# V projected for two units at a time, in high and low parts, in the decoder's local-attention stack

## The chip, the cores and the metric

One core of a Trainium2 chip runs the whole program. The metric is the device time of one execution in microseconds (us), lower is better; the time before is the median of three runs.

## The reference

The program is one decoder step: a state-space and expert block, a cross attention, and then a stack of six layers. All of the change is in the stack. Cut to what matters, a layer of the stack is:

```python
def attn_layer(x, Wqkv, qs, ksc, Wo):            # x: (2, 512, 128), 16 heads of 64
    q, k, v = jnp.split(x @ Wqkv, 3, -1)         # each split in 16 heads
    q = l2norm(q) * qs; k = l2norm(k) * ksc
    q = q * cos * scale + rotate_half(q) * sin * scale
    k = k * cos * inv + rotate_half(k) * sin * inv
    out = local_attention(q, k, v)               # windows of 32, each looks at itself and the one before
    return out @ Wo

for i in range(6):
    x = attn_layer(shift_tokens(x), ...) + x
    x = ffn_layer(shift_tokens(x), ...) + x      # layer norm, a * gelu(gate), W2
```

`v = x @ Wv` is 512x128 by 128x1024 for each of the two sequences, in every layer. This product is what is computed in another way.

## The kernel before

Activations lie transposed, channels on the 128 partitions and the 512 positions of a sequence along the free dimension (`Y`, called `stream` in the trace). The work of a layer is cut in 16 units: unit n is sequence n // 8 and head pair n % 8. All engines run the same software pipeline, `body(s)`, one step t at a time (t = 0 to 15 in a layer; -4 to -1 fill it at the start). Each engine works through its own list in program order and waits on semaphores (`Flow`; `at(turn, n)` is the n-th event of a turn, which is a layer). In step t the engines do, among other things:

- TensorE (L1376): the scores of unit t+1 (L1299, L1305), the projection of Q and K for unit t+4 (`project`, L1254), the transposes of the probabilities of unit t (L1317), the output projection of unit t-1 (L1339), the V projection of unit t+1 (`project_v`, L1280), the sum of squares of the heads of t+4 (`head_norm`, L1273, into `NORM_BANK`), and probabilities times V of unit t (`values`, L1320).
- ScalarE (L1468): the squares of unit t+4 (L1420), the exponential, two copies of probabilities (L1451), the copy of V to SBUF (`copy_v`, L1453), logarithm and root of the norm, the copy of the output.
- VectorE (L1594): row maximum and subtraction (L1604, L1610), the multiplication with the norm (`normalise_heads`, L1550, output `st_turned`), in some steps the rounding of a weight (`high_weights`, L1527), in some steps parts of the feed-forward block, then the two rotary products (`rotate`, L1539, L1540), the row sum and the reciprocal (L1632, L1636).
- GpSimd, called POOL (L1658): the sum of two squares (L1667, output `st_sq_sum`, which `head_norm` waits for), the two rotary sums (L1671, L1672), the normalised probabilities (L1679, `pn`, shown as `mo_w<-st_prob,st_ri`, which the transposes of the next step wait for), and in some steps the low part of a weight (`low_weights`, L1654).
- SyncE (SP, L1215): the DMAs. `place_heads` puts Q (4 DMAs) or K (8 DMAs, `st_k_blocks`) of unit t+3 in place, `shift_values` makes a copy of V shifted by 32 positions, `st_vs`, with 2 DMAs for each unit; weights of the next layer are loaded in chosen steps.

Names in the trace are those of the buffers: `st_sq_sum`, `st_turned`, `st_w_high` and so on; `h` is `sq`, `x` with 128x1024 is `sin_part`, `mo_w` stands for `cos_part` and `pn`, which lie in a buffer of an earlier part, and `banks` is PSUM.

Q and K are projected in three passes of a faster one-pass format (`F32R`, fp32r in the trace): the weight and `Y` are each split in a rounded high part and the remainder, and high times high, low times high and high times low are added in PSUM (L1266 to L1270). The splitting of `w_raw` is done ahead, one eighth i in step t = i + 7 of the layer before (for the first layer in the steps -4 to 2): VectorE rounds (L1530), POOL subtracts (L1656). V is projected in plain fp32 from `Y` and `wv`, a unit at a time: four matmuls, each with 128 positions as output rows and 128 columns (L1290); the hardware runs each as two passes, so the trace shows eight.

The feed-forward block of one sequence lies in the steps 0 to 3 (for sequence 1 of the layer before) and 8 to 11 (for sequence 0): stage 0 adds the attention output (`residual1`, L1558) and takes the mean (L1343) and variance (L1347), stage 1 the first gate products, stage 2 the two value products L1369 ahead of the transposes, stage 3 the last products and `down` (L1374). It borrows `V_BANK` for some products, so `project_v` waits for `act_done` in the stages 2 and 3.

## Time and profile before

| what | value |
|---|---|
| median of 3 runs | 1370.93 us |
| lowest and highest of them | 1365.84 and 1378.49 us |
| the profiled execution's own time | 1366.57 us |
| its span, first to last instruction | 1363.8 us |
| the stack, first projection to the end of its pipeline | 395.2 to about 1320 us |
| TensorE busy | 1174.1 us (86%) |
| VectorE, ScalarE, POOL busy | 942.8, 838.3, 658.7 us |
| mean granted TensorE clock | 0.948 |

The time outside the span is 2.8 us in the profiled execution. The busy time of an engine is a sum over the whole program; whether an engine is the bound is read from what its neighbours wait for. A row of the timeline gives the start, the duration, the engine, the line, output <- input, and in brackets the idle time in front of it and what ended that.

### The profile page before, as it was taken

Reading aid. Unit: us, or ns where it says so; the run is one execution under the profiler, and the core shown is the slowest. Engines: PE = TensorE matmul, PEld = TensorE weight load, DVE = VectorE, ACT = ScalarE, POOL = GpSimd, SP = SyncE. Lnnn points to the kernel's source line nnn. Section 1 sums busy time; section 2 is a strip of 40 time slices with the busy share of each in tenths; the row PEclk is TensorE's granted clock in tenths of the full one; section 3 lists DMA queues with packets and bytes.
Section 4 is the critical chain, followed back from the end, with each engine's and each line's share of the span. In section 5 each row is a group of like instructions: output and inputs, shape, how many; then the busy total and the mean of one; then the engine's idle time right before and its main releaser. Section 6 shows DMA issues by size and latency. Waiting matters only on the chain. (4 is left out here: it accounts for less than half of the span.)

```text
span 1363.8 us, 26023 instructions
## 1 busy us (share of the span) xinstructions
PE 1174.1 (86%) x9636; PEld 726.5 (53%) x9636; DVE 942.8 (69%) x1207; ACT 838.3 (61%) x1260; POOL 658.7 (48%) x522
## 2 busy tenths in 40 slices
PE   7787869998557988898889989999888989999975
PEld 3222347786224655566555655656555655656551
DVE  2788957775736776776777767767776776767733
ACT  4553456664345668675776667775776767676744
POOL 1555524442326555645555555645555555555420
PEclk9887989999868999999999999999999999999997
DMA  3000035100203532444233432444233432434220
GB/s 106 1 0 0 1 48 193 46 24 1 92 14 87 134 96 68 111 114 108 69 96 98 124 94 74 109 116 112 69 96 96 122 98 74 106 92 108 73 58 16
DMA packets 75507, 107.08 MB, mean 79 GB/s; under 512 B 25347, under 2 KB 31938, under 8 KB 75002
## 3 DMA queue, kind: packets, MB, share of 16 engines
q1 hardware_dynamic: 75386, 105.47, 29.8%
q8 instruction: 76, 1.25, 0.4%
q14 instruction: 45, 0.37, 0.1%
HBM read 30.89 MB, written 0.59 MB: 23 GB/s over the span
## 5 line engine op out<-in xcount | busy, mean ns | idle before, releaser
L1667 POOL TENSOR_TENSOR st_sq_sum<-h 128x512 f32<-128x512 f32 x96 | 127.3, 1327 | 235.1 <-ACT h L1420 235.1
L1604 DVE TENSOR_REDUCE st_mx<-banks 128x8 f32<-128x512 f32 x96 | 66.4, 692 | 201.4 <-PE banks L1305 201.1
L1671 POOL TENSOR_TENSOR mo_w<-mo_w,x 128x512 f32<-128x512 f32 x96 | 122.1, 1272 | 160.1 <-DVE mo_w L1540 160.1
L1420 ACT ACTIVATE h<-banks 128x1024 f32<-128x1024 f32 x96 | 98.4, 1025 | 157.8 <-PE banks L1270 157.5
L1278 PE MATMUL banks<-st_sq_sum,head_ones 128*128 128x512 f32 x192 | 108.4, 647 | 41.5 <-POOL st_sq_sum L1667 41.5
L1290 PEld LDWEIGHTS banks<-st_wv,stream 128*128 128x128 f32 x768 | 102.3, 194 | 48.4 <-issue 47.8
L1539 DVE TENSOR_TENSOR x<-banks,st_scaled 128x1024 f32<-128x1024 f32 x96 | 117.0, 1219 | 14.3 <-ACT h L1420 12.8
L1550 DVE SCALAR_TENSOR_TENSOR st_turned<-st_rn,mo_w 128x1024 f32<-128x1024 f32 x96 | 120.9, 1259 | 5.4 <-ACT st_rn L1431 2.8
L1672 POOL TENSOR_TENSOR mo_w<-mo_w,x 128x512 f32<-128x512 f32 x96 | 122.2, 1272 | 0.0
L1329 PEld LDWEIGHTS banks<-st_p_blocks,st_vs 128*64 128x64 f32 x1536 | 77.8, 137 | 74.0 <-issue 72.6
L1540 DVE TENSOR_TENSOR mo_w<-banks,st_scaled 128x1024 f32<-128x1024 f32 x96 | 116.5, 1213 | 0.0
L1451 ACT ACTIVATE st_p_blocks<-banks 64x512 f32<-64x512 f32 x192 | 112.5, 586 | 3.2 <-PE banks L1317 0.8
L430 POOL TENSOR_TENSOR ma_dbx<-ma_u,ma_b_rows 128x1024 f32<-128x1024 f32 x32 | 75.4, 2361 | 79.4 <-ACT ma_b_rows L288 54.8
L1679 POOL TENSOR_TENSOR mo_w<-st_prob,st_ri 128x512 f32<-128x512 f32 x96 | 100.1, 1043 | 17.0 <-DVE st_ri L1636 17.0
L1305 PE MATMUL banks<-st_k_blocks,st_qT 128*32 128x128 f32 x3072 | 107.7, 282 | 0.0
L1266 PE MATMUL banks<-st_y_high,st_w_high 128*128 128x512 f32 x192 | 90.9, 473 | 18.6 <-issue 10.0
L1339 PE MATMUL banks<-x,st_wo 128*128 128x512 f32 x192 | 102.5, 616 | 0.8 <-ACT x L1444 0.8
L1290 PE MATMUL banks<-st_wv,stream 128*128 128x128 f32 x768 | 102.9, 278 | 0.0
L1329 PE MATMUL banks<-st_p_blocks,st_vs 128*64 128x64 f32 x1536 | 99.4, 228 | 2.6 <-ACT st_p_blocks L1451 2.6
L1427 ACT ACTIVATE st_rn<-banks,fill 128x512 f32<-128x512 f32 x96 | 66.1, 688 | 52.2 <-PE banks L1278 52.2
L1305 PEld LDWEIGHTS banks<-st_k_blocks,st_qT 128*32 128x32 f32 x3072 | 80.7, 112 | 32.4 <-issue 32.1
L1329 PE MATMUL banks<-st_p_blocks,st_vn 128*64 128x64 f32 x1536 | 94.8, 222 | 0.0
(230 smaller groups left out, 2656.1 us busy)
## 6 DMA issues: line engine op xcount, KB each, us to landing
st_qT<-st_turned SPq DMA_DIRECT2D x192, 128.0 KB, 2.4
st_k_blocks<-st_turned SPq DMA_DIRECT2D x384, 64.0 KB, 2.0
st_vs<-st_vn SPq DMA_DIRECT2D x96, 192.0 KB, 2.5
st_w_raw<-in_w_qk SPq DMA_DIRECT2D x12, 512.0 KB, 4.7
st_vs<-st_vn SPq DMA_DIRECT2D x96, 48.0 KB, 2.1
mo_w_all<-gate_rows SPq DMA_DIRECT2D x1, 3072.0 KB, 13.2
st_wv<-in_w_v SPq DMA_DIRECT2D x12, 256.0 KB, 3.0
st_wo<-in_wo SPq DMA_DIRECT2D x12, 256.0 KB, 3.1
```

Of the source, the lines that this page charges most:

```text
L1278: mm(NORM_BANK, C["head_ones"], sq_sum[:], start=True, stop=True).then_inc(norm_done.sem, 1)
L1290: last = mm(V_BANK[:, rows], Y[:, b, rows], wv[:, pair, :], start=True, stop=True)
L1305: last = mm(SCORE_BANK[rows].rearrange("p (o h i k) -> p o h i k", o=2, h=2, i=2)[:, odd, :, i, :], qT[:, r, pair, t0:t0 + WIN], k_blocks[ ...
L1329: last = mm(TURN_BANK[rows, P * j:P * j + P].rearrange("p (h o q) -> p h o q", h=2, q=WIN)[:, :, odd, :], (vn if odd else vs)[:, r, j, row ...
L1339: mm(OUT_BANK[b], wo[:, pair, :], oT[:, n % 2, :], start=(pair == 0), stop=(pair == 7)).then_inc(wo_step.sem, 1)
L1451: A(p_blocks[rows, r, half, :], TURN_BANK[rows, :], ACT.Copy).then_inc(pt_copied.sem, 1)
L1539: v.tensor_tensor(sin_part[:], QK_BANKS, scaled[:, which, 1], ALU.mult).then_inc(product_done.sem, 1)
L1540: v.tensor_tensor(cos_part[:, which], QK_BANKS, scaled[:, which, 0], ALU.mult).then_inc(product_done.sem, 1)
L1550: v.scalar_tensor_tensor(turned[:, h % 4], rn[:, h % 2, :].unsqueeze(1).to_broadcast([P, 2, SEQ]), 1e12, cos_part[:, which], ALU.min, ALU. ...
L1667: nc.gpsimd.tensor_tensor(sq_sum[:], sq[:, 0, :], sq[:, 1, :], ALU.add).then_inc(sq_summed.sem, 1)
L1671: nc.gpsimd.tensor_tensor(cos_part[:, which, 0, :], cos_part[:, which, 0, :], sin_part[:, 1, :], ALU.subtract).then_inc(add_done.sem, 1)
L1672: nc.gpsimd.tensor_tensor(cos_part[:, which, 1, :], cos_part[:, which, 1, :], sin_part[:, 0, :], ALU.add).then_inc(add_done.sem, 1)
```

## The change

- V is projected in the high and low parts too: three F32R matmuls take the place of each fp32 one, with `y_high` and `y_low` as the stationary operand and `wv_high`, `wv_low` as the moving one.
- It is done for two units (a pair, four heads, 256 columns) at a time. A step now computes half the positions (two blocks of 128) for both units of the pair, so a step has six matmuls with 256 columns. V of the pair 2g, 2g+1 is computed in the steps 2g-2 and 2g-1, one step earlier than before for the even unit's first half.
- `copy_v` copies one half in each step, into `vn` with two units side by side; `shift_values` runs in odd steps only, with two DMAs of double size.
- The V weights are split as the others: four `tensor_copy` of 128x256 on VectorE and four subtractions on POOL for each layer, right behind those of the Q and K weights of odd i. In the layers' pipeline these are the steps 8, 10, 12 and 14; for the first layer the steps -4, -2, 0 and 2.
- The V weights are loaded in one DMA in step 3, not in two in the steps 11 and 15. Three buffers move to space of an earlier part.

The diff, cut to its core:

```diff
@@ SyncE
         def shift_values(s, n):
-            r = n % 2
-            sp.wait_ge(*v_copied.at(s.turn, n + 1))
+            r = n // 2 % 2
+            sp.wait_ge(*v_copied.at(s.turn, n + 2))
             sp.dma_start(vs[32:128, r, :, :], vn[0:96, r, :, :]).then_inc(vs_in[r].sem, 16)
             sp.dma_start(vs[0:32, r, 1:4, :], vn[96:128, r, 0:3, :]).then_inc(vs_in[r].sem, 16)
...
-                if t >= -1 and s.unit(t + 1):
+                if t >= -1 and t % 2 == 1 and s.unit(t + 1):
                     shift_values(s, t + 1)
...
-                        sp.wait_ge(*w_split.at(turn, PARTS))
+                        sp.wait_ge(*w_split.at(turn, SPLITS))
                         for half in range(2):
                             places.load_qk(sp, d, turn + 1, half)
+                        places.load_v(sp, d, turn + 1)
...
-                    if t == 11:
-                        sp.wait_ge(*v_done.at(turn, 12))
-                        places.load_v(sp, d, turn + 1, 0)
...
-                    if t == 15:
-                        sp.wait_ge(*v_done.at(turn, 16))
-                        places.load_v(sp, d, turn + 1, 1)
@@ TensorE
         def project_v(s, n, job, stage):
-            b, pair = n // 8 % 2, n % 8
+            b, g, half = n // 8 % 2, n % 8 // 2, n % 2
...
-            pe.wait_ge(*wv_in[pair // 4].at(s.turn, 16 * (n // 16) + 16))
-            for tile in range(4):
-                rows = slice(P * tile, P * tile + P)
-                last = mm(V_BANK[:, rows], Y[:, b, rows], wv[:, pair, :], start=True, stop=True)
+            if n % 16 < 8 and half == 0:
+                pe.wait_ge(*w_split.at(s.turn, SPLITS * (n // 16) + v_split(g)))
+            if n % 8 == 0:
+                pe.wait_ge(*y_low_done.at(s.turn, n // 8 + 1))
+            for i in range(2):
+                rows = slice(P * (2 * half + i), P * (2 * half + i) + P)
+                out = V_BANK[:, 2 * P * i:2 * P * i + 2 * P]
+                mm(out, y_high[:, b, rows], wv_high[:, g, :], start=True, stop=False)
+                mm(out, y_high[:, b, rows], wv_low[:, g, :], start=False, stop=False)
+                last = mm(out, y_low[:, b, rows], wv_high[:, g, :], start=False, stop=True)
             last.then_inc(v_done.sem, 1)
...
         def values(s, n):
-            r = n % 2
-            pe.wait_ge(*vs_in[r].at(s.turn, 32 * (n // 2) + 32))
+            r, q = n % 2, n // 2 % 2
+            pe.wait_ge(*vs_in[q].at(s.turn, 32 * (n // 4) + 32))
...
-                if t >= -1 and s.unit(t + 1):
-                    project_v(s, t + 1, job, stage)
+                if t >= -2 and s.unit(t + 2):
+                    project_v(s, t + 2, job, stage)
@@ ScalarE
         def copy_v(s, n):
-            r = n % 2
+            r, half = n // 2 % 2, n % 2
             ac.wait_ge(*v_done.at(s.turn, n + 1))
...
-            A(vn[:, r], V_BANK.rearrange("p (j f) -> p j f", f=P), ACT.Copy).then_inc(v_copied.sem, 1)
+            A(vn[:, r, 2 * half:2 * half + 2, :], V_BANK.rearrange("p (j f) -> p j f", f=2 * P), ACT.Copy).then_inc(v_copied.sem, 1)
@@ VectorE
             v.tensor_copy(w_high[:, i, :], w_raw[:, i, :]).then_inc(w_high_done.sem, 1)
+            if i % 2 == 1:
+                g = i // 2
+                dv.wait_ge(*places.wv_in.at(s.turn, 16 * ahead + 16))
+                if ahead:
+                    dv.wait_ge(*v_done.at(s.turn, 10 + 2 * g))
+                v.tensor_copy(wv_high[:, g, :], wv_raw[:, g, :]).then_inc(w_high_done.sem, 1)
@@ GpSimd
-            pool.wait_ge(*w_high_done.at(s.turn, PARTS * ahead + i + 1))
+            pool.wait_ge(*w_high_done.at(s.turn, SPLITS * ahead + qk_split(i)))
             nc.gpsimd.tensor_tensor(w_low[:, i, :], w_raw[:, i, :], w_high[:, i, :], ALU.subtract).then_inc(w_split.sem, 1)
+            if i % 2 == 1:
+                g = i // 2
+                pool.wait_ge(*w_high_done.at(s.turn, SPLITS * ahead + v_split(g)))
+                nc.gpsimd.tensor_tensor(wv_low[:, g, :], wv_raw[:, g, :], wv_high[:, g, :], ALU.subtract).then_inc(w_split.sem, 1)
```

Where the instructions stand. TensorE, the middle of a plain step, before: the last of the six Q and K matmuls, transposes, output projection, V, and the sum over a head.

```order
L1270 MATMUL banks<-st_y_low,st_w_high 128x512
L1317 MATMUL banks<-ident,mo_w 128x128 x4
L1339 MATMUL banks<-x,st_wo 128x512
L1290 MATMUL banks<-st_wv,stream 128x128 x4
L1278 MATMUL banks<-st_sq_sum,head_ones 128x512
```

The same place in the changed kernel, where the lines have moved by a few:

```order
L1272 MATMUL banks<-st_y_low,st_w_high 128x512
L1325 MATMUL banks<-ident,mo_w 128x128 x4
L1348 MATMUL banks<-x,st_wo 128x512
L1296 MATMUL banks<-st_wv_high,st_y_high 128x256
L1297 MATMUL banks<-st_wv_low,st_y_high 128x256
L1298 MATMUL banks<-st_wv_high,st_y_low 128x256
L1296 MATMUL banks<-st_wv_high,st_y_high 128x256
L1297 MATMUL banks<-st_wv_low,st_y_high 128x256
L1298 MATMUL banks<-st_wv_high,st_y_low 128x256
L1280 MATMUL banks<-st_sq_sum,head_ones 128x512
```

V stays between the output projection and the sum over a head; only its form changes. GpSimd, the end of step 14 and step 15 of a layer, before (`st_w_low` is the last eighth of the Q and K weights, the next row the squares' sum of step 15):

```order
L1679 TENSOR_TENSOR mo_w<-st_prob,st_ri 128x512
L1656 TENSOR_TENSOR st_w_low<-st_w_raw,st_w_high 128x256
L1667 TENSOR_TENSOR st_sq_sum<-h 128x512
L1671 TENSOR_TENSOR mo_w<-mo_w,x 128x512
L1672 TENSOR_TENSOR mo_w<-mo_w,x 128x512
```

The same place in the changed kernel:

```order
L1699 TENSOR_TENSOR mo_w<-st_prob,st_ri 128x512
L1672 TENSOR_TENSOR st_w_low<-st_w_raw,st_w_high 128x256
L1676 TENSOR_TENSOR st_wv_low<-st_wv_raw,st_wv_high 128x256
L1687 TENSOR_TENSOR st_sq_sum<-h 128x512
L1691 TENSOR_TENSOR mo_w<-mo_w,x 128x512
L1692 TENSOR_TENSOR mo_w<-mo_w,x 128x512
```

The subtraction for V stands between the one for Q and K and the next sum of squares. The same holds for the steps 8, 10 and 12, and for the steps -4, -2, 0 and 2 of the first layer.

## Rows read from the trace of the kernel before

**Rows 1.** Waits over the whole span: who waited for whom, us in total, times, longest.

```profile
POOL st_sq_sum L1667 <- ACT h L1420: 235.1, 86, 6.5
PE banks L1278 <- POOL st_sq_sum L1667: 41.5, 81, 2.5
PE banks L1299 <- DMA st_k_blocks<-st_turned: 17.1, 21, 2.0
```

**Rows 2.** Timeline of TensorE, step 14 of the third layer: start, duration, work, idle.

```profile
861.82 0.50 PE L1266 MATMUL banks<-st_y_high,st_w_high 128*128 128x512 f32 x1
...
863.32 0.60 PE L1317 MATMUL banks<-ident,mo_w 128*128 128x128 f32 x4
...
864.62 1.05 PE L1290 MATMUL banks<-st_wv,stream 128*128 128x128 f32 x8
865.95 1.12 PE L1278 MATMUL banks<-st_sq_sum,head_ones 128*128 128x512 f32 x2 [0.28 <-POOL st_sq_sum L1667]
868.62 0.39 PE L1299 MATMUL banks<-mask,ident 128*128 128x512 bf16 x1 [0.46 <-DMA st_k_blocks<-st_turned]
```

**Rows 3.** Timeline of ScalarE, the same step.

```profile
863.52 1.02 ACT L1420 ACTIVATE h<-banks 128x1024 f32<-128x1024 f32 x1 [2.08 <-PE banks L1270]
```

**Rows 4.** Timeline of TensorE, step 10 of the same layer.

```profile
826.94 1.05 PE L1290 MATMUL banks<-st_wv,stream 128*128 128x128 f32 x8
827.83 1.02 PE L1278 MATMUL banks<-st_sq_sum,head_ones 128*128 128x512 f32 x2
```

**Rows 5.** The weight rounding's line over the span: count, then ns min/median/max.

```profile
L1530 DVE CAST st_w_high<-st_w_raw x48: 280/287/1385, 394.0 to 1171.4; 128x256 fp32r<-128x256 f32 x48
```

**Rows 6.** Timeline of VectorE, step 14.

```profile
863.29 1.44 DVE L1550 SCALAR_TENSOR_TENSOR st_turned<-st_rn,mo_w 128x1024 f32<-128x1024 f32 x1
864.66 1.39 DVE L1530 CAST st_w_high<-st_w_raw 128x256 fp32r<-128x256 f32 x1
865.97 1.21 DVE L1539 TENSOR_TENSOR x<-banks,st_scaled 128x1024 f32<-128x1024 f32 x1
```

**Rows 7.** Timeline of POOL, and one row of TensorE, steps 14 and 15.

```profile
864.62 1.27 POOL L1667 TENSOR_TENSOR st_sq_sum<-h 128x512 f32<-128x512 f32 x1 [0.97 <-ACT h L1420]
...
871.87 1.71 POOL L1656 TENSOR_TENSOR st_w_low<-st_w_raw,st_w_high 128x256 fp32r<-128x256 f32 x1
873.54 1.27 POOL L1667 TENSOR_TENSOR st_sq_sum<-h 128x512 f32<-128x512 f32 x1
...
871.96 0.66 PE L1317 MATMUL banks<-ident,mo_w 128*128 128x128 f32 x4 [0.35 <-POOL mo_w L1679]
```

**Rows 8.** Timeline of POOL and VectorE, end of step 12 and step 13.

```profile
854.75 0.72 POOL L1656 TENSOR_TENSOR st_w_low<-st_w_raw,st_w_high 128x256 fp32r<-128x256 f32 x1
857.02 1.28 POOL L1667 TENSOR_TENSOR st_sq_sum<-h 128x512 f32<-128x512 f32 x1 [1.54 <-ACT h L1420]
...
855.68 1.22 DVE L1550 SCALAR_TENSOR_TENSOR st_turned<-st_rn,mo_w 128x1024 f32<-128x1024 f32 x1
```

**Rows 9.** Timeline of VectorE and TensorE, step 8 of the first and third layer.

```profile
493.33 1.37 DVE L1530 CAST st_w_high<-st_w_raw 128x256 fp32r<-128x256 f32 x1
...
804.07 0.28 DVE L1530 CAST st_w_high<-st_w_raw 128x256 fp32r<-128x256 f32 x1
...
496.07 1.13 PE L1343 MATMUL banks<-stream,mean_ones 128*128 128x512 f32 x2 [0.35 <-DVE stream L1558]
```

**Rows 10.** Timeline of POOL and TensorE, step -2 of the first layer.

```profile
413.65 1.27 POOL L1667 TENSOR_TENSOR st_sq_sum<-h 128x512 f32<-128x512 f32 x1
...
414.98 1.12 PE L1278 MATMUL banks<-st_sq_sum,head_ones 128*128 128x512 f32 x2 [2.54 <-POOL st_sq_sum L1667]
```

**Rows 11.** DMA issues: KB each, median us to landing; then SP's timeline, step 13.

```profile
st_vs<-st_vn SPq DMA_DIRECT2D x96, 192.0 KB, 2.5
st_w_raw<-in_w_qk SPq DMA_DIRECT2D x12, 512.0 KB, 4.7
...
859.38 0.60 SPq L1212 DMA_DIRECT2D st_vs<-st_vn  x1
```

More of the change, by code:

```diff
@@ L1048, in __init__ @@
         self.p_blocks = sb("p_blocks", [P, 2, 2, SEQ])
-        self.qT, self.vs = sb("qT", [P, 2, 2, SEQ]), sb("vs", [P, 2, 4, P])
+        self.qT, self.vs = sb("qT", [P, 2, 2, SEQ]), sb("vs", [P, 2, 4, 2 * P])
         self.proj_in = flow("proj_in", 32)
-        self.wv_in = [flow(f"wv_in_{i}", 16) for i in range(2)]
+        self.wv_in = flow("wv_in", 16)
         self.wo_in = [flow(f"wo_in_{i}", 16) for i in range(2)]
@@ L1076, in load_first @@
             self.load_qk(sp, d, 0, half)
-            self.load_v(sp, d, 0, half)
+            if half == 0:
+                self.load_v(sp, d, 0)
             self.load_wo(sp, d, 0, half)
@@ L1327, in values @@
                         rows = slice(64 * head, 64 * head + 64)
+                        cols = slice(P * r + 64 * head, P * r + 64 * head + 64)
                         at = P * (2 * odd + head) + WIN * j
                         last = mm(TURN_BANK[rows, P * j:P * j + P].rearrange("p (h o q) -> p h o q", h=2, q=WIN)[:, :, odd, :],
-                                  (vn if odd else vs)[:, r, j, rows], p_blocks[:, r, :, at:at + WIN],
+                                  (vn if odd else vs)[:, q, j, cols], p_blocks[:, r, :, at:at + WIN],
                                   start=True, stop=True)
@@ L1354, in up_gate @@
             if j == 1:
[L1355 removed]
+                pe.wait_ge(*v_copied.at(s.turn, min(t + 3, UNITS) if s.last else t + 3))
             if j == 2:
@@ L1485, in body @@
                     copy_probs(s, t)
-                if t >= -1 and s.unit(t + 1):
-                    copy_v(s, t + 1)
+                if t >= -2 and s.unit(t + 2):
+                    copy_v(s, t + 2)
                 if s.unit(t + 4):
@@ L1796, in program @@
         with ExitStack() as part:
-            spare = (x[:], h1[:], x1[:], weights.all[:].rearrange("p e g c -> p (e g) c"))
+            spare = (x[:], h1[:], x1[:], weights.all[:].rearrange("p e g c -> p (e g) c"), cross.place["bias"][:].rearrange("p t h k -> p t (h k)"),
+                     (cross.onehot[:, 0:SEQ], cross.line[:, 0:SEQ]))
             build_stack(nc, part, Y, stack, spare, d, C)
```

63 lines of the change are left out of this document (33 added, 30 removed).

## The prediction

> **What bounds the kernel now.** I read three views in this order: the waits over the whole span, to find which engine waits for which; the timeline of one plain step, to see what ends last in it; and the timelines of the steps in which weights are split, since only there is work added.
>
> The waits show TensorE standing before the sum over a head (L1278) for POOL's sum of squares, 81 times in 96, and before the scores (L1299) for the K transfer, 21 times [rows 1]. TensorE is the busiest engine, but in most steps it is not the bound; a chain through three engines is. In step 14 the six Q and K matmuls start at 861.82 and the next work at 863.32 [rows 2]. ScalarE squares from 863.52 for 1.02 [rows 3], POOL sums from 864.62 for 1.27 [rows 7], and the head sum starts at 865.95 [rows 2]: 2.63 us after the projection has ended, whatever TensorE does in between. What it does is transposes, output projection and V. V begins at 864.62, and the head sum could follow it after 0.89, as it does in step 10, where nothing is waited for (826.94 to 827.83) [rows 4]. It follows after 1.33. So 0.44 us of each such step is already lost in front of the head sum, and a shorter V only makes this wait longer. The plain steps have the same pattern, 0.28 us of it shown as idle. In even steps a second chain, from the scores over VectorE's multiplication (L1550) and the K transfers to the next scores, ends last: the scores of step 15 start 0.46 us late for it [rows 2]. V is not in it either.
>
> **The change part by part.** The sum is made against the profiled execution, 1366.57 us (span 1363.8 and 2.8 around it); the median of the runs is 4.4 higher.
>
> 1. V on TensorE. The six Q and K matmuls with 512 columns take 863.32 - 861.82 = 1.50 us [rows 2]. Six with 256 columns are half of it, 0.75, if the time goes with the columns, against 0.89 for fp32 [rows 4]: 0.14 less. It counts only where the head sum does not wait: stage 2 of the feed-forward block, whose two extra products lie inside the chain (steps 2 and 10, 12 in all), and step 12 in the five layers where TensorE runs behind at the low clock: 17 x 0.14 = 2.4 us gained. The bounds: no gain at all, or a matmul as short as an fp32 pass of today (0.89/8 = 0.11, six are 0.67, 17 x 0.22 = 3.7). The other side, in which 256 columns cost as much as 512, is a rival below.
> The Trainium skill (TensorE: Matmul & The Clock Gate, Back-to-back issue gap) puts a 256-column matmul at 262 cycles, 0.109 us at 2.4 GHz, which would make six 0.66 us, the step 0.23 shorter, and this term 3.9 in place of 2.4; no row here has a 256-column matmul in this format.
>
> 2. Step 8 (five layers). The rounding of a weight is 0.29 us (287 ns median) but up to 1385 ns [rows 5]: when POOL's sum of squares has just started, the rounding stands until it ends. In step 14 POOL runs from 864.62 for 1.27, and the rounding that began at 864.66 took 1.39 [rows 6, 7]. In step 8 it is the same in four of five layers (1.37 at 493.33) and not in the third (0.28 at 804.07) [rows 9]. Behind the rounding come the residual, which the mean product waits for (0.35 idle [rows 9]), the centring, the variance: this is the path. The second rounding adds 0.2 (distance of two in a row: 0.29 less an overlap of 0.09) where the first was caught anyway, and in the third layer it is caught itself, 1.3: 4 x 0.2 + 1.3 = 2.1 us lost. Bounds 0 and 5 x 1.4.
>
> 3. Steps 14 and 15 (five layers). In step 14 the rotary products start with the end of the rounding (865.97 [rows 6]) and through POOL's sums and normalised probabilities set when the transposes of step 15 start: those wait already, 0.35 us idle [rows 7]. So +0.2 to 0.3 there. Then POOL's weight subtraction (871.87, 1.71 long, since it stands while VectorE multiplies) runs right up to the sum of squares at 873.54 [rows 7]; no gap is left. The added subtraction is another 0.72 [rows 8], all of it in front of that sum, and the head sum of step 15 waits for it. Together about 1.0 per layer; one layer of the five has a late DMA there which gives slack: 4.5 us lost. Bounds 0 and 6.
>
> 4. Steps 12 to 14. POOL's subtraction in step 12 ends at 855.47, 1.54 ahead of the next sum of squares [rows 8]: 0.72 more fits, but it then runs to 856.19 and over the start of VectorE's multiplication at 855.68 [rows 8]. The two shut each other out, as the 1.71 and the 1.44 (1.22 when alone) of step 14 show [rows 6, 7, 8]. The multiplication ends 0.5 later, at 857.4, past the time at which POOL's sum wants to start (857.02). That costs 0.2 on the head sum; and if the rounding of step 13 is then caught behind the sum, 1.3 on the rotary products. Value 0.5 per layer, 2.5 us; bounds 0 and 2.5 per layer.
> The Trainium skill (SBUF — State Buffer, SBUF: two separate sides) says why: the port pair that VectorE and GpSimd share is an exclusive lock, taken for the whole instruction by a VectorE copy in a two-port mode or with two SBUF inputs. The trace agrees (1.39 against 0.29). The rule speaks against this change, since all that it adds to both engines is of the kinds that lock.
>
> 5. The fill of the pipeline. In the first layer the subtraction stands directly before the sum of squares, which starts as it ends (413.65), and TensorE waits 2.54 for that [rows 10]. In the steps -2, 0 and 2 there is one more, 0.72 each: 2.2 us lost. In step -4 it lies ahead of the first squares. Bounds 0 and 3.
>
> 6. Steps 10: one more rounding before two feed-forward products with room behind them: 0, or 0.2 each where the room is gone.
>
> 7. Copy, shift, loads. The copies stay 96 of the same size in the same place of ScalarE's list, and in the plain steps they stand behind the probability copies, not behind V: 0. The shift in odd steps grows from 192 KB, which lands after 2.5 us, to 384 KB; 512 KB take 4.7 [rows 11]. Issued at 859.38 it is due for `values` of step 14, after the head sum of 865.95 and its 0.95: seven microseconds. 0, or a wait of 1 us in the feed-forward steps if the queue is full. SP issues 96 DMAs less, but none of them stood before a K transfer that was late. V's load moves behind the others of step 3, and the K transfers of step 4 come about 6 us after those: 0, bound 1 us in each of five layers.
>
> The sum: -2.4 + 2.1 + 4.5 + 2.5 + 2.2 = +8.9, so 1375.5 in the profiled execution. With the 4.4 by which the median stood above it: 1379.9; I say 1379.
>
> The K transfers have a luck of their own. The longest wait for them is 2.0 us [rows 1], it comes in five or so steps, and other instruction counts will move it: +-5 us.
>
> **The rivals.**
>
> A. Slower, the cascade of step 12. The late multiplication makes the rounding of step 13 lose to POOL's sum in every layer, the rotary products start 1.5 late, the probabilities come after the transposes of step 14 want them, and the same engines meet again in step 14. For it: losing costs 1.1 us (1.39 against 0.28), and the margin is some hundredths. Against: the wait in front of the head sum (0.44) and that for K (0.46) absorb some 0.9 of each. It decides if the multiplication of step 13 ends after ScalarE's squares. Price 2.5 in place of 0.5 per layer: 10 more, 1389.
>
> B. Slower, 256 columns cost as 512. Then V takes 1.50: 0.61 more in the 17 bound steps, 0.17 more (1.50 - 1.33) in about 70 waiting ones, 22 in all with the gain gone: 1402. For it: no row shows the form; the time of a small matmul may be set by its weights. Against: an fp32 pass with the same weight load repeats after 0.11 [rows 4].
>
> C. Within noise, the splits are hidden. The locks fall better than in the present trace and only term 1 and half of term 5 stay: 1366.6 - 2.4 + 1 + 4.4 = 1370.
>
> D. Faster, V is on the path after all: the chain in front of the head sum gets shorter with it, for instance since POOL or ScalarE start earlier. 96 x 0.14 = 13 us: 1358, with 0.22 1350. Against it are the equal waits in all plain steps.
>
> **How the numbers follow.** Forecast 0.44, A 0.22, B 0.06, C 0.21, D 0.07. A measurement of this kernel tells about 1% from no change, that is 1357.2 and 1384.6. The forecast (1372 to 1386 by itself) is nine tenths in the middle; A is slower in nine of ten; B slower; C the same; D half faster. Slower: 0.04 + 0.20 + 0.06 = 0.30. Faster 0.04. Same 0.66. The range takes in C and A and leaves out most of B and D: 1363 to 1394.
>
> **What would show it.** The V group: about 0.75 us from its start to the end of the last, the idle time in front of the head sum in plain steps up from 0.28 to about 0.42, and the length of plain steps unchanged. In the steps 2 and 10 the head sum follows V after 0.75. In step 15 a head sum later by 0.7 and transposes by 0.2. The roundings of the V weight at 0.2 to 0.3, one in five at 1.4. The waits on POOL's sum, 41.5 in all today [rows 1], would rise by some 15. The forecast is wrong if plain steps get shorter (D), if the V group takes over 1.2 us (B), if the transposes of step 14 wait over 1 us (A), or if `values` waits for the shifted V.

## The result, and the profile after

| | before | changed kernel |
| --- | --- | --- |
| median of 20 runs each | 1368.2 us | 1377.29 us |
| lowest to highest | 1362.09 to 1378.49 | 1370.72 to 1383.44 |
| span of the profiled execution | 1363.8 | 1375.4 |
| ratio after / before | | 1.0066, interval 1.0049 to 1.0083 |

The change costs 9 us between the medians. It lies within 1%, as the prediction's likeliest case had it (1379, range 1363 to 1394). Which parts of its sum were right is another question.

The waits over the whole span, changed kernel (who waited for whom, us in total, times, longest):

```profile
POOL st_sq_sum L1687 <- ACT h L1429: 222.1, 81, 7.4
PE banks L1280 <- POOL st_sq_sum L1687: 59.8, 75, 3.2
PE banks L1313 <- DMA st_k_blocks<-st_turned: 26.9, 21, 3.8
```

TensorE's wait in front of the head sum rose from 41.5 to 59.8 [rows 1], 18 more where 15 were forecast. The wait for K rose from 17.1 to 26.9, and the longest of these from 2.0 to 3.8; the prediction's sum put that at nothing.

V itself, on TensorE's timeline in step 10 of the third layer:

```profile
836.29 0.36 PE L1296 MATMUL banks<-st_wv_high,st_y_high 128*128 128x256 f32 x1
836.48 0.28 PE L1297 MATMUL banks<-st_wv_low,st_y_high 128*128 128x256 f32 x1
836.60 0.28 PE L1298 MATMUL banks<-st_wv_high,st_y_low 128*128 128x256 f32 x1
...
836.96 0.28 PE L1298 MATMUL banks<-st_wv_high,st_y_low 128*128 128x256 f32 x1
837.08 1.02 PE L1280 MATMUL banks<-st_sq_sum,head_ones 128*128 128x512 f32 x2
```

The starts are 0.12 us apart. From the first to the head sum it is 0.79, against 0.89 before [rows 4]. In a plain step nothing of this shows. Here is the head sum of step 6 in the third layer; the kernel before has 0.28 in the brackets, at 786.66:

```profile
795.08 1.13 PE L1280 MATMUL banks<-st_sq_sum,head_ones 128*128 128x512 f32 x2 [0.47 <-POOL st_sq_sum L1687]
```

The wait took 0.2 us more, where the prediction had 0.14 (0.28 to 0.42).

The best measure of where the time went is the distance from the start of one head sum (L1278 before, L1280 after) to the start of the next, read from TensorE's timeline. Interval t runs from the head sum of step t to that of the next step, so work of step t+1 ahead of its head sum lies in interval t. Summed over the layers in us; before and after are each a mean over three profiled executions (the kernel, and the two placements of it among the experiments, e6 and e10, e7 and e11):

| intervals | before | after | difference |
| --- | --- | --- | --- |
| fill, -4 to 2 of the first layer | 55.8 | 58.7 | +2.9 |
| 3, 5, 6, 7 | 201.8 | 202.3 | +0.4 |
| 4, first layer alone | 8.0 | 13.0 | +5.0 |
| 4, the other five | 44.5 | 43.5 | -1.1 |
| 8 | 78.9 | 79.5 | +0.6 |
| 9, 10 | 120.2 | 119.8 | -0.4 |
| 11, 12 | 107.5 | 110.8 | +3.3 |
| 13, 14, 15 | 121.4 | 124.0 | +2.6 |
| 0, 1, 2 | 158.5 | 158.1 | -0.4 |
| all | 896.5 | 909.5 | +13.0 |

One execution scatters by some 3 us either way (893.5 to 900.3 for the three of before, 906.6 to 913.3 of after), so 13.0 is no contradiction to 9.1 between the medians. One reason for the difference is that the profiled execution of e11 was the longest of its five (1391.87 us, median 1387.38). The plain intervals (5, 7, 15) did not move: 7.60 before, 7.61 after.

**The splits.** Timelines of VectorE and POOL and the head sum on TensorE, changed kernel, around step 12 of the fifth layer, then of the third:

```profile
1167.10 1.37 DVE L1540 CAST st_w_high<-st_w_raw 128x256 fp32r<-128x256 f32 x1
1168.39 0.28 DVE L1546 CAST st_wv_high<-st_wv_raw 128x256 fp32r<-128x256 f32 x1
1168.59 1.21 DVE L1555 TENSOR_TENSOR x<-banks,st_scaled 128x1024 f32<-128x1024 f32 x1
1166.98 1.34 POOL L1687 TENSOR_TENSOR st_sq_sum<-h 128x512 f32<-128x512 f32 x1 [5.72 <-ACT h L1429]
1168.37 1.12 PE L1280 MATMUL banks<-st_sq_sum,head_ones 128*128 128x512 f32 x2 [0.53 <-POOL st_sq_sum L1687]
...
857.68 0.29 DVE L1540 CAST st_w_high<-st_w_raw 128x256 fp32r<-128x256 f32 x1
857.88 0.28 DVE L1546 CAST st_wv_high<-st_wv_raw 128x256 fp32r<-128x256 f32 x1
858.08 1.22 DVE L1555 TENSOR_TENSOR x<-banks,st_scaled 128x1024 f32<-128x1024 f32 x1
857.93 1.36 POOL L1687 TENSOR_TENSOR st_sq_sum<-h 128x512 f32<-128x512 f32 x1 [6.08 <-ACT h L1429]
859.93 1.02 PE L1280 MATMUL banks<-st_sq_sum,head_ones 128*128 128x512 f32 x2
```

In the fifth layer POOL's sum began at 1166.98, 0.12 ahead of the rounding, and the rounding stood until it ended: 1.37 in place of 0.29. Such a rounding is called caught here. The rotary product starts 0.22 after the head sum (1168.37). In the third layer both roundings began before POOL's sum, and the product starts 1.85 ahead of the head sum (859.93). The intervals that follow are 9.89 and 7.75. These 2.1 us are not all loss: the interval in front, 11, was 12.52 in the fifth layer and 13.50 in the third, so the head sum of step 12 itself stood about 1 us sooner. The two intervals have to be read together: 22.41 against 21.25, so the catch cost 1.16. In the kernel before they are 21.1 to 21.2 without a catch and 21.5 to 21.6 with one, if layers with a late K transfer are left out, so there a catch cost 0.4. Over three executions of each kernel a rounding in step 12, of either weight, was caught in 4 of 15 cases before and in 11 of 15 after.

The two lengths of interval 11 go with TensorE's granted clock. Stretches of the span, changed kernel, over this interval in the third layer and in the fifth (each engine's busy time, then the granted clock, the DMA share, GB/s):

```profile
846.40:859.90 13.50, 11.23 (x91) 6.91 (x92) 8.83 (x14) 8.04 (x12) 5.55 (x5) 0.87 0.29 75
1155.80:1168.40 12.60, 9.80 (x92) 5.98 (x92) 7.93 (x12) 7.94 (x12) 5.52 (x5) 1.00 0.28 71
```

In all 14 traces of this document, 70 such intervals, it is 12.5 us where the granted clock stayed at 1.00 and 12.9 to 13.7 where it was 0.87 or 0.88 in the mean. It stayed up in 24 of them, and in all 24 the first rounding of step 12 was caught. So this clock sets in part in which phase the two engines meet in step 12. It stayed up in 3 of 15 cases before and in 6 of 15 after; why in these is open.

**The fill.** POOL's timeline in step -3, changed kernel:

```profile
411.29 0.73 POOL L1672 TENSOR_TENSOR st_w_low<-st_w_raw,st_w_high 128x256 fp32r<-128x256 f32 x1 [2.39 <-DVE st_w_high L1540]
411.98 0.73 POOL L1676 TENSOR_TENSOR st_wv_low<-st_wv_raw,st_wv_high 128x256 fp32r<-128x256 f32 x1
412.67 1.26 POOL L1687 TENSOR_TENSOR st_sq_sum<-h 128x512 f32<-128x512 f32 x1
```

The added subtraction stands in front of the sum that TensorE waits for, behind the one that already stood there. Interval -3 went from 7.17 to 7.86 and interval 1 from 8.45 to 9.15, by 0.69 each, the subtraction's distance.

**The loads.** SyncE's timeline in the first layer, kernel before:

```profile
456.95 0.60 SPq L1212 DMA_DIRECT2D st_vs<-st_vn  x1
457.59 0.60 SPq L1213 DMA_DIRECT2D st_vs<-st_vn  x1
458.24 1.07 SPq L1059 DMA_DIRECT2D st_w_raw<-in_w_qk  x2
459.35 1.67 SPq L1070 DMA_DIRECT2D st_rope_scale<-in_rope_scale  x1
462.09 4.98 SPq L1207 DMA_DIRECT2D st_k_blocks<-st_turned  x8
```

The same in the changed kernel:

```profile
459.31 0.59 SPq L1219 DMA_DIRECT2D st_vs<-st_vn  x1
459.94 0.60 SPq L1220 DMA_DIRECT2D st_vs<-st_vn  x1
460.58 1.19 SPq L1059 DMA_DIRECT2D st_w_raw<-in_w_qk  x2
461.81 0.43 SPq L1062 DMA_DIRECT2D st_wv_raw<-in_w_v  x1
462.29 0.72 SPq L1069 DMA_DIRECT2D st_rope_scale<-in_rope_scale  x1
464.46 5.97 SPq L1214 DMA_DIRECT2D st_k_blocks<-st_turned  x8
```

The K transfer follows the start of the loads by 3.9 us in both, but the shift in front of them is twice as large (384 and 96 KB, not 192 and 48) and 512 KB of V weights have come between. What the engines did next in the changed kernel, first TensorE's timeline, then stretches of the span (each engine's busy time, then the granted clock, the DMA share, GB/s):

```profile
471.93 1.94 PE L1313 MATMUL banks<-st_k_blocks,st_qT 128*32 128x128 f32 x32 [3.83 <-DMA st_k_blocks<-st_turned]
...
474.39 0.63 PE L1269 MATMUL banks<-st_y_high,st_w_low 128*128 128x512 f32 x1
474.81 0.63 PE L1272 MATMUL banks<-st_y_low,st_w_high 128*128 128x512 f32 x1
...
466.00:470.00 4.00, 2.10 (x34) 1.20 (x34) 1.65 (x3) 2.57 (x5) 3.07 (x3) 1.00 0.86 275
470.00:474.00 4.00, 2.07 (x33) 1.70 (x35) 0.07 (x1) 0.00 (x0) 0.44 (x1) 0.52 0.22 57
474.00:478.00 4.00, 4.00 (x13) 2.90 (x13) 2.63 (x4) 1.24 (x2) 0.14 (x1) 0.63 0.08 18
```

The K transfer shared the DMA engines with the tail of the loads (275 GB/s up to 470), the scores waited 3.83 us, and behind this pause the granted clock stood at 0.52 and 0.63, that is mostly at 1.2 GHz, so that the Q and K matmuls came 0.42 apart in place of the 0.25 of step 14 [rows 2]. The lower level was granted from 470.2 to 477.0; in the kernel before the granted clock was 1.00 from 460 to 476. The one interval grew from 7.98 to 13.31 for both reasons; how much belongs to each was not measured apart. In later layers interval 3 lasts 10.45 and not 7.6, since feed-forward work stands in it. There 6.0 to 7.2 us lie between the loads and the K transfer, the Q and K weights have landed or have at most 1.2 us to go, and the first of the eight K DMAs takes 1.9 to 2.5 us from issue to landing. In the first layer it takes 4.3 (2.4 in the kernel before).

The page's DMA issues after (KB each, median us to landing), beside [rows 11]:

```profile
st_vs<-st_vn SPq DMA_DIRECT2D x48, 384.0 KB, 3.5
st_w_raw<-in_w_qk SPq DMA_DIRECT2D x12, 512.0 KB, 5.8
st_wv_raw<-in_w_v SPq DMA_DIRECT2D x6, 512.0 KB, 7.4
```

### The profile page after: what moved, and what is told of

It reads as the page before. It is cut to its first block and busy times, and to the rows that moved or that the text cites. A ratio compares the mean times of both kernels' runs of the same rounds, so it can differ in the third digit from the quotient of the medians.

```text
span 1375.4 us, 25414 instructions
## 1 busy us (share of the span) xinstructions
PE 1135.5 (83%) x9349; PEld 708.0 (51%) x9444; DVE 953.8 (69%) x1231; ACT 838.7 (61%) x1260; POOL 682.0 (50%) x546
## 5 line engine op out<-in xcount | busy, mean ns | idle before, releaser
L1280 PE MATMUL banks<-st_sq_sum,head_ones 128*128 128x512 f32 x192 | 109.0, 650 | 60.6 <-POOL st_sq_sum L1687 59.8
L1313 PE MATMUL banks<-st_k_blocks,st_qT 128*32 128x128 f32 x3072 | 109.1, 285 | 43.7 <-DMA st_k_blocks<-st_turned 26.9
L1566 DVE SCALAR_TENSOR_TENSOR st_turned<-st_rn,mo_w 128x1024 f32<-128x1024 f32 x96 | 124.2, 1294 | 6.1 <-ACT st_rn L1440 3.5
L1296 PE MATMUL banks<-st_wv_high,st_y_high 128*128 128x256 f32 x192 | 87.4, 455 | 1.7 <-DVE cr_bias L1607 1.7
L370 DVE TENSOR_TENSOR_SCAN ma_state<-banks,ma_dbx 128x512 f32<-128x512 f32 x64 | 76.2, 1212 | 17.2 <-ACT banks L298 14.6
```

The costliest lines, as they stand in the source:

```text
L1280: mm(NORM_BANK, C["head_ones"], sq_sum[:], start=True, stop=True).then_inc(norm_done.sem, 1)
L1313: last = mm(SCORE_BANK[rows].rearrange("p (o h i k) -> p o h i k", o=2, h=2, i=2)[:, odd, :, i, :], qT[:, r, pair, t0:t0 + WIN], k_blocks[ ...
L1566: v.scalar_tensor_tensor(turned[:, h % 4], rn[:, h % 2, :].unsqueeze(1).to_broadcast([P, 2, SEQ]), 1e12, cos_part[:, which], ALU.min, ALU. ...
```

## The experiments

Twelve kernels ran, in three groups of four, with runs of the kernel before beside each group (medians 1366.9, 1368.0, 1368.1). Ratios are against those. The changed kernel itself did not run beside the groups, so a difference to it is that of two ratios, known to about 4 us either way; intervals are read from one execution of each kernel.

**e1_load_v_step6.** Only the V load is moved.

```diff
                     if t == 3:
...
-                        places.load_v(sp, d, turn + 1)
...
+                    if t == 6:
+                        places.load_v(sp, d, turn + 1)
```

> The changed kernel with the load of the V weights moved from step 3 (behind the two Q and K weight loads) to step 6, behind its K transfers. Theory 1, the load is in the way: in the first layer step 3 is short, 1.5 MB are still under way when the K transfers of step 4 are issued, and the scores of step 5 wait 3.9 us for them; without the V load the stretch from the head sum of step 4 to that of step 5 goes from 13.3 back to about 8, in later layers by up to 1; in all 5 to 7 us faster than the changed kernel (1377.3), so 1370 to 1372, ratio to before about 1.002. Theory 2, luck of the K transfers: that stretch moves anywhere, no change of the median within 2 us.

Measured: 1378.66, ratio 1.0088 (1.0061 to 1.0115). Interval 4 of the first layer fell from 13.3 to 11.2, not to 8.0, and the rest of the span was no shorter; intervals 8 and 12 were at 82.4 and 47.3. One execution is thin for this, since the same interval is 11.8 and 13.8 in e11 and e7 with no load moved. Taken together, it is 11.8 to 14.2 in the six executions with V's load behind the others in step 3 (the changed kernel, e2, e3, e4, e7, e11; mean 13.4), and 11.2, 11.3 and 9.3 with it elsewhere (e1, e9, e12; mean 10.6). So the V load is about half of the loss, and the total of e1 showed nothing of it.

**e2_splits_moved.** The V splits leave the steps of the Q and K splits: all four in step -4 for the first layer; for a later layer in the steps 9 and 11, and 0 and 1 of the layer itself.

```diff
-    def v_split(g):
-        return 3 * g + 3
+    V_FIRST, V_LATER = [-4, -4, -4, -4], [9, 11, 16, 17]
```

> The changed kernel with the V weight splits (rounding on VectorE and subtraction on GpSimd) in other steps: all four in step -4 for the first layer, and in the steps 9, 11 and the next layer's 0 and 1 later on, where GpSimd has 2 to 6 us before its next sum of squares. Theory 1, the splits of the steps 8, 12 and 14 cost by the locks: 4 us back in the fill of the pipeline, 5 to 7 us back in the steps 8 and 11 to 15, together about 8 to 10 of 1377.3, so 1367 to 1369, ratio 1.000. Theory 2, what costs is work on VectorE as such, or the new form of V: no more than 3 us back.

Measured: 1371.89, ratio 1.0035 (1.0012 to 1.0057), 4 to 5 us better than the changed kernel, half of the 8 to 10 expected. No rounding was caught in step 12; the intervals 11 and 12 took 105.5 (after 110.8), 13 to 15 took 121.9 (124.0), the fill 56.5 (58.7). Interval 9 rose from 10.62 to 11.69 in the five layers with a split in it, 5.4 us in all, but interval 8 fell by as much (74.4 after 79.5), so the two together stayed as they were. The price of the splits depends on the step in which they stand.

**e3_splits_tiny.** The splits for the second to the last layer touch 2 columns in place of 256, which leaves the rest of these weights' high and low parts out.

```diff
-                v.tensor_copy(wv_high[:, g, :], wv_raw[:, g, :]).then_inc(w_high_done.sem, 1)
+                    v.tensor_copy(wv_high[:, g, 0:2], wv_raw[:, g, 0:2]).then_inc(w_high_done.sem, 1)
...
+                c = 2 if ahead else 2 * P
+                nc.gpsimd.tensor_tensor(wv_low[:, g, 0:c], wv_raw[:, g, 0:c], wv_high[:, g, 0:c], ALU.subtract).then_inc(w_split.sem, 1)
```

> The changed kernel with the V weight splits of the layers 2 to 6 cut to 2 of 256 columns (so V is computed from the first layer's weights but for these); all waits and places stay. Theory 1: the 5 to 7 us that the steps 8 and 11 to 15 cost over before shrink to the fixed cost of a tiny instruction, 4 to 6 us faster than 1377.3, so 1371 to 1373, ratio 1.003. Theory 2, the form of V or the DMAs cost: no change within 2 us.

Measured: 1373.48, ratio 1.0046 (1.0023 to 1.0068). By the ratios this is 2.7 us under the changed kernel, which is not clear of the noise; the intervals say more. Intervals 11 and 12 took 107.9, all but what they took before (107.5), and interval 9 10.50 in place of 10.62; 13 to 15 stayed high, at 123.6. The fill and interval 4 of the first layer (13.47), in which nothing was cut, stayed at the changed kernel's values. VectorE's timeline in step 12 of the third layer:

```profile
852.37 1.37 DVE L1540 CAST st_w_high<-st_w_raw 128x256 fp32r<-128x256 f32 x1
853.66 0.16 DVE L1546 CAST st_wv_high<-st_wv_raw 128x2 fp32r<-128x2 f32 x1
```

A copy of two columns is nearly free, and still the first rounding was caught in four layers of five. The intervals 11 and 12 of these layers took 21.7 together, against 21.0 in the fifth and 22.4 for a caught layer of the changed kernel. These four layers are also those in which the granted clock stayed at 1.00 in interval 11. So in step 12 the size of what was added did not decide whether the first rounding is caught, only what that costs.

**e4_v_one_pass.** V from the high parts alone; the two products with a low part are left out.

```diff
-                mm(out, y_high[:, b, rows], wv_high[:, g, :], start=True, stop=False)
-                mm(out, y_high[:, b, rows], wv_low[:, g, :], start=False, stop=False)
-                last = mm(out, y_low[:, b, rows], wv_high[:, g, :], start=False, stop=True)
+                last = mm(out, y_high[:, b, rows], wv_high[:, g, :], start=True, stop=True)
```

> The changed kernel with one of V's three passes (high times high): two matmuls of 256 columns in a step, not six; the splits stay. Theory 1, a chain over ScalarE and GpSimd sets the head sum: 0.5 us of TensorE's time less in each of 96 steps gives only 17 x 0.4 = 7 us at most, in the steps 2, 10 and 12; the idle time before the head sum in plain steps goes up from 0.42 to about 0.9. So 1370 to 1376. Theory 2, V is on TensorE's path: 96 x 0.45 = 43 us, 1334.

Measured: 1376.25, ratio 1.0068 (1.0043 to 1.0094), as much as the changed kernel and just above what theory 1 said, though four of six V matmuls are gone. TensorE's waits there:

```profile
PE banks L1280 <- POOL st_sq_sum L1685: 97.6, 81, 3.1
```

The wait took up most of what V gave back (59.8 to 97.6). The intervals 1 and 9, in which V is on the path, fell to 10.04 and 10.15 (from 10.50 and 10.62); 5 and 7 stayed at 7.60. But 13 and 15 grew (43.0 and 41.0 over the layers, after 39.4 and 38.1), and so did the fill (62.0 after 58.7). An earlier V seems to change the phase of the other engines too; that was not followed further.

**e5_loads_in_step4.**

```diff
-                    if t == 3:
+                    if t == 4:
```

> The changed kernel with the loads that SyncE issues in step 3 (q and K weights, V weights, scale of the next layer) issued in step 4 instead, behind that step's K transfers. Theory 1 (in step 4 of the first layer the K transfer shares the DMA engines with the tail of a larger load, 1 MB where the kernel before had one weight block in the first place): the interval from the head sum of step 4 to the next in the first layer falls from 13.3 to about 8.0 us, step 4 over all layers from 56.0 to about 50 us, everything else stays, time 5 us below the changed kernel, 1372. Theory 2 (the lateness there comes from the instruction-fetch packet, 1.2 us on one DMA engine in the same window): the interval stays at 9 or more, the sum of step 4 falls by at most 2, time 1375. If the loads now hit the K transfer of step 5 in their turn, step 5 rises by up to 4 us in the first layer and the time stays at 1377.

Measured: 1385.09, ratio 1.0122 (1.0085 to 1.0159). Interval 4 of the first layer fell to 7.92: theory 1 was right on that place. But interval 6 rose from 51.0 to 61.4 over the layers, and the time by 8 us. The text named step 5 as the next victim with 4 us; it was 6 with 10, in five layers, not in one (5 and 7 stayed at 7.61). (The loads are 1.5 MB in the changed kernel and 1 MB before; the texts of e5 and e9 say less.)

**e6_before_fetch_shift** and **e10_before_shift_half** (the kernel before), **e7_after_fetch_shift** and **e11_after_shift_half** (the changed one), with 64 and 128 more semaphore instructions on TensorE:

```diff
-        pe.wait_ge(pads_zero.sem, 3)
+        for _ in range(128):
+            pe.wait_ge(pads_zero.sem, 3)
         all_turns(pe, body)
```

(two of these make one instruction; 256 in e10 and e11).

> The kernel before, with 64 more semaphore instructions on TensorE ahead of the stack's first matmul, where it is idle for 8.6 us; they wait for a semaphore that has its value already, and nothing else differs. Theory (which K transfers come late is decided by where TensorE's instruction-fetch packets of 16 KB fall, and these fall by the number of instructions ahead): the late transfers are at other steps than in the kernel before (there: step 12 of the first layer, 4 of the second, 6 of the third, 4 of the fourth, 14 of the fifth, sum about 7 us without that of step 0), and the time moves by up to 5 us either way, 1363 to 1372, though no work of the stack has changed. Rival (lateness belongs to the transfers and the loads beside them): the same steps are late by the same amounts, and the time is within 1 us of before.

> The changed kernel with the same 64 semaphore instructions on TensorE. Theory (instruction-fetch packets decide the lateness): late transfers at other steps than in the changed kernel, and a time between 1371 and 1380; the 13.3 us of step 4 in the first layer, which also has the loads in its window, falls to between 9 and 12. The steps that the change itself made dearer (12 by 0.5 in each undisturbed layer, the fill by 3) stay as they are. Rival: the same intervals as in the changed kernel within 0.3 each, time 1377 within 1.

> The kernel before with 128 more semaphore instructions on TensorE ahead of the stack (e6 had 64 and took 1371.5 against 1368.0). Theory (the place of the fetch packets is a matter of luck of 2 to 4 us either way): between 1365 and 1373, with late K transfers at other steps than in either. Rival (the instructions themselves cost, 64 of them 3.5 us, since they run in TensorE's queue ahead of the stack): 1375, and the stack's first head sum stands 7 us later.

> The changed kernel with 128 more semaphore instructions on TensorE (64 gave 1381.3, none 1377.3). Theory: between 1374 and 1382; step 4 of the first layer at 13 to 14 us once more (loads), step 12 near 45 in all, the fill 3 above before, since these belong to the change and not to the place of the fetch packets. The mean of the changed kernel over its three placements lies 8 to 12 us above the mean of the kernel before over its three. Rival (the change costs nothing itself and 1377 was an unlucky placement): 1371 or less here.

Measured: e6 1371.45 (1.0025, 1.0005 to 1.0045), e10 1375.71 (1.0053, 1.0026 to 1.0080), e7 1381.32 (1.0101, 1.0076 to 1.0126), e11 1387.38 (1.0132, 1.0088 to 1.0176). The times rise with the number of instructions, as the rival in e10's text had it (1375), and e7, e10 and e11 lie above what the theory gave them (at most 1380, 1373 and 1382). TensorE's first matmul of the stack, in e6 and then in e10:

```profile
395.61 0.77 PE L1266 MATMUL banks<-st_y_high,st_w_high 128*128 128x512 f32 x1 [11.49 <-issue]
...
404.37 0.77 PE L1266 MATMUL banks<-st_y_high,st_w_high 128*128 128x512 f32 x1 [18.38 <-issue]
```

It stood idle for 8.6 before the change of placement; now for 11.5 and 18.4. The instructions themselves had become the bound there, so e6 holds 2.9 us of lead and e10 9.8; in e7 and e11 these are 2.4 (11.3 against 8.9) and 9.3 (18.2). Without them the medians are

| | as it is | 64 more | 128 more | mean |
| --- | --- | --- | --- | --- |
| before | 1368.2 | 1368.6 | 1365.9 | 1367.6 |
| after | 1377.3 | 1378.9 | 1378.1 | 1378.1 |

The late transfers did move: of the intervals 4, 6, 12 and 14, those above 11 us were 4 of the second layer, 6 of the third and 14 of the fifth in before, 12 of the second and 6 of the sixth in e6, and none in e10. The median hardly followed. So the placement is worth about 1.5 us either way, and the change 9.1, 10.3 and 12.2 us in the three placements, 10.5 in the mean. The fetch theory falls as a cause of the result. Interval 4 of the first layer came out at 13.8 in e7 (9 to 12 was expected) and 11.8 in e11 (13 to 14 was expected), against 8.0 in all three of before. In neither e7 nor e11 did an instruction packet of 16 KB run while this K transfer was under way, so its lateness belongs to the loads and the shift in front of it.

**e8_splits_and_loads.** As e2, with other steps for the splits, and the loads as in e5.

```diff
+    V_FIRST, V_LATER = [-4, -4, -4, -4], [10, 11, 17, 17]
...
-                    if t == 3:
+                    if t == 4:
```

> The changed kernel with the splits of the V weights taken off step 12: in the first layer all in step -4, in later ones the first in step 10, the second in step 11, the third and fourth in step 1 of the next layer (of the kernel's numbering), and the loads of step 3 issued in step 4. Theory: step 12 stays near 8.0 per layer (39 to 40 in all), the first layer's step 4 near 8.0, step 9 back to 62.9 (it was 68.3 with a split in it), steps 10 and 11 rise by at most 1 in all, the roundings' 4 x 0.2 and more go from step 8: time 1367, between 1362 and 1372 by the luck of the K transfers. Rival (each split costs its 0.5 to 1 us wherever it stands, since VectorE's slack in every step is less than that): steps 10, 11 and 1 rise by 1 per layer and split, 15 in all, and the time is 1375.

Measured: 1372.44, ratio 1.0028 (1.0012 to 1.0045), just above what was expected. Interval 4 of the first layer was 7.90, interval 9 63.6 as in the changed kernel, 10 and 11 no dearer than there (the text's 62.9 and 68.3 for step 9 are read from the second matmul of the head sum, which makes them 0.6 less). Interval 12 took 41.0 (after 45.3), a little more than expected. Step 1 cost 0.4 per layer (10.90 against 10.50) and interval 6 54.9 against 51.0.

**e9_loads_apart** and **e12_loads_apart_shift** (the same with 64 more semaphore instructions).

```diff
+                    if t == 2:
+                        sp.wait_ge(*vw_split.at(turn, 4))
+                        places.load_v(sp, d, turn + 1)
-                    if t == 4:
+                    if t == 3:
```

> The kernel of e8_splits_and_loads with its loads apart: the V weights of the next layer issued by SyncE in step 2 of its list, the Q and K weights and the scale in step 3, as before the change. Theory (in e8 the 1 MB of loads issued at once only moved from the K transfer of step 4 to that of step 6): step 4 of the first layer stays at 8.0 us, or 9.5 with a fetch packet, and step 6 falls from 54.9 to between 49 and 52 over the layers; time 1369, between 1365 and 1373 by the luck of the fetch packets, so 3 below e8. Rival (the tail of step 6 in e8 was fetch packets alone): step 6 does not fall by more than 2, and the time stays at 1372.

> The kernel of e9_loads_apart with 64 more semaphore instructions on TensorE. Theory: the same structure with another placement of the fetch packets, 1365 to 1373; the mean of e9 and this one lies within 2 us of the mean of the kernel before over its three placements (about 1370), since the V matmuls give 2 to 3 us back and the splits in steps 10, 11 and 1 cost about 2. Rival (the new order of splits and loads beats the kernel before): the mean is 1367 or less.

Measured: e9 1367.07, ratio 1.0001 (0.9972 to 1.0030); e12 1371.99, ratio 1.0028 (0.9999 to 1.0056), of which 2.8 are the instructions. The mean without these is 1368.1, level with before and 9 to 10 us under the changed kernel. (The profiled execution of e9 was the longest of its twelve, 1376.63, so its intervals say less about its median than those of the others.) Interval 6 fell to 50.2 and 49.2, so theory held against the rival; interval 4 of the first layer was 11.3 and 9.3, where 8.0 to 9.5 was expected. V's load is out of the way there, as in e1; what is left in front of the Q and K weights, against before, is the shift of double size. That the shift does it was not tried by itself. A packet of 16 KB ran beside this K transfer in e1 and e9 and none in e12, which may be the 2 us between their 11.2 and 11.3 and its 9.3.

## Why the prediction was right, and where it was not

The total, 1379 for 1377.3, is a hit; the sum has one term missing and two in the wrong place.

**Term 1, V on TensorE, -2.4.** The group came to 0.79 (0.75 forecast). In interval 1, where no split stands, the gain is 0.18 per layer (10.68 to 10.50); in interval 9 it is 0.18 with the tiny splits of e3 and in the last layer, which has none, and 0.06 with the real ones; in 11 0.18 (13.67 to 13.49). That is 5 x 0.18 + 5 x 0.06 + 0.18 + 5 x 0.18 = 2.3 at most. The reason held too: e4 took two thirds of V away and the plain intervals stayed at 7.60, so D falls, and a spacing of 0.12 ends B. (B's price was added up wrongly: 0.75 more against the forecast's 0.75 group in 17 steps, and 0.17 in 70, make 24.7, so 1404 or 1405 and not 1402. It changes nothing in the range. And the prediction took all five layers to run at the low clock ahead of step 12; before the change it was 12 of 15.)
The 0.66 us that followed from the Trainium skill (TensorE: Matmul & The Clock Gate, Back-to-back issue gap) is short of the trace: 0.12 us apart, not 0.109, and 0.79 for the group with the first matmul's 0.19.

**Term 2, step 8, +2.1.** Measured +0.6 in the means, +0.21 in undisturbed layers (12.89 to 13.10, the 0.2 forecast). The 1.3 for a layer in which nothing is caught was too much: of 15 such cases before only one was free.

**Terms 3 and 4, steps 14 and 15, +4.5, and 12 to 14, +2.5.** Together 7.0; measured 3.3 + 2.6 = 5.9 in the intervals 11 to 15, 6.8 with V's gain taken off. The sum is about right and its parts are not: term 3 came to 1.2 of its 4.5 (intervals 14 and 15), term 4 to 4.7 in place of 2.5 (11 to 13). That these errors cancel is luck. The failing step of term 3 was to take "all of it in front of that sum, and the head sum of step 15 waits for it" for all layers but one. Where a rounding was caught in step 14, the interval rose from 8.92 to 9.6 or 9.8, which is the price that the prediction gave. But in 7 of 15 layers nothing was caught there (8.33 in most of them; before, a rounding was caught in 14 of 15). In all seven a rounding had been caught in step 12 already, so it seems that the loss falls in one place or the other. Interval 15 stayed at 7.61. Step 12 paid more than 0.5: 1.16 for a catch, in 11 of 15 layers. This is a loss of A's kind, but not where A put it: in step 13 a rounding stood its full 1.36 in only 2 of 15 layers, and interval 13 grew by 1.4 us over the five. e2 takes the splits out of step 12 and the loss goes; e3 cuts their size and intervals 11 and 12 lose most of it.
The exclusive lock of the Trainium skill (SBUF — State Buffer, SBUF: two separate sides) is borne out once more: 0.29 against 1.37 with POOL's sum begun 0.12 earlier.

**Term 5, the fill, +2.2.** Measured +2.9; 0.69 in each of intervals -3 and 1 is the subtraction, the other intervals vary by 1 to 2 us between executions.

**Term 6, step 10, 0 or 0.2 each:** 0.13 each.

**Term 7, loads, 0 with a bound of 1 us per layer:** this is the step that failed. That "the K transfers of step 4 come about 6 us after those" holds in the later layers (6.4 to 7.2 before the change). In the first layer they come after 3.9, behind a shift of double size, and the term is +5.0, all in one place, a part of it by the lower clock behind the pause. The other five layers showed no loss. e5 and e8 bring the interval back to 7.9; e1, e9 and e12 together put V's load at about half of it, and the rest, which points to the shift, was not tried by itself.

**Other signs.** In the changed kernel's trace 4 of the 24 roundings of a V weight were caught (one in five was named), the transposes never waited over 0.9 us for POOL, and `values` never waited for the shifted V.

**The luck of the K transfers, +-5 us:** about 3 from one execution to the next, and about 1.5 in the median.

So the total came out right though 5 us were missing, and that is partly luck. The forecast added 8.9; the medians give 9.1, the intervals 13.0, which is 4 more. There, the 5.0 of the loads and 0.7 of the fill that were missing are set against step 8, 1.5 too dear, and the later layers' interval 4, 1.1 shorter; smaller differences make up the rest. The absolute 1379 was helped besides by its start: the median of before, which the forecast took at 1370.93 from three runs, is 1368.2 over twenty, 2.7 lower. C, the hidden splits, is nearer to e9, which puts them where they hide, than to this kernel.

## What to carry to other kernels

Work that is added to two engines which shut each other out is priced by the phase in which it meets the other, not by its length alone: read where each starts in the step, and move it to a step in which the other is free (e2: 4 to 5 us for the same instructions; with the loads apart as well, e9 and e12, 9 to 10). A load that is moved must be followed in the shortest step that it can fall in, here the first layer's, and up to the next transfer that something waits for; moving it by one step found the next victim. And shortening a matmul group that ends ahead of a wait gives that wait its time, nothing else.

## What the runs showed of the hardware that was not expected

- Semaphore waits that are already met are not free in a row: between e6 and e10, 64 more took the idle time before the stack's first matmul from 11.49 to 18.38, 0.108 us each, and the median of the whole run rose by 4.3.
- A pause of 3.8 us in TensorE cost more than itself: from 470 to 478 us, over it and behind it, the granted clock was 0.52 to 0.63, with the lower level from 470.2 to 477.0.
- Call a K transfer of eight DMAs late if it takes over 0.5 us more than the median of its trace from first issue to last landing (medians 6.7 in before, 6.8 in the changed kernel, 6.5 in e5). All 14 late ones in before, all 10 in the changed kernel and all 19 in e5 have a packet of 16 KB of the instruction queue (75 on the changed kernel's page) running 0.9 to 1.6 us on one of the 16 DMA engines at the same time. Of those that were not late, 13 of 34, 20 of 38 and 9 of 29 have one too, so such a packet beside a transfer does not always make it late. Nor is it the only cause: in e7 the K transfer of the first layer's step 4 was late with none beside it. Which steps are late moved with 64 more instructions. It looks like a cause of most single late transfers, but no run took such a packet away, so it stays a reading of the trace.
